# A decoder's second loop: metric scores in four 32-row tiles, and its orders rewritten

## The reference, cut to what matters

```python
metric_nkk = jnp.einsum('nij,nkj->nik', pre_metric_nkk, pre_metric_nkk)
proj_bwc = in_sequence_bwc @ W_proj.T
proj_bnwk = proj_bwc.reshape(b, w, N, K).transpose(0, 2, 1, 3)
qm_bnwk = jnp.einsum('bnwk,nkj->bnwj', proj_bnwk, metric_nkk)
scores_bnww = jnp.einsum('bnwk,bnvk->bnwv', qm_bnwk, proj_bnwk) / math.sqrt(K)
scores_bnww = scores_bnww * mask_ww          # lower triangle
nudged_bnwk = jnp.einsum('bnwv,bnvk->bnwk', scores_bnww, proj_bnwk)
nudged_bnwk = jnp.einsum('bnwk,nkj->bnwj', nudged_bnwk, transforms_nkk)
return nudged_bnwk.transpose(0, 2, 1, 3).reshape(b, w, c) @ W_mixer.T
```

## Time and profile before

| | |
|---|---|
| three runs | 1551.40, 1548.36, 1551.33 us, median 1551.33 |
| profiled execution | 1548.21 us, its span 1546.4 us |
| busy share of the span | PE 87%, PEld 57%, DVE 68%, ACT 34%, POOL 18% |
| TensorE's mean granted clock | 0.927 |
| largest lines of the chain that ended last | L824 10%, L1040 7%, L1099 6%, L934 6%, L759 4%, L988 4% |

### The profile page before, as it was taken

The page is one execution under the profiler, slowest core; times in us unless marked ns, Lnnn a source line. Parts: engine busy times, 40 slices in busy tenths (PEclk is TensorE's granted clock), DMA queues, the critical chain, the costliest instruction groups (busy, mean ns, idle before and its releaser), DMA issues.

```text
span 1546.4 us, 17959 instructions
## 1 busy us (share of the span) xinstructions
PE 1338.6 (87%) x7004; PEld 882.2 (57%) x7004; DVE 1052.5 (68%) x2018; ACT 523.8 (34%) x602; POOL 283.1 (18%) x188
## 2 busy tenths in 40 slices
PE   7999999988699997852276999999999999999874
PEld 4666676666444445421153567675757667666663
DVE  4688888863333336978724487787969788777774
ACT  2333333332233336966310323222333313232410
POOL 0111111110000001005400032323214032313240
PEclk9999999985799998975588999999999999999986
DMA  4000000000153211379612202011020200010000
GB/s 180 15 14 28 28 28 28 14 15 14 64 223 109 95 81 52 125 262 335 246 55 89 76 14 75 28 48 55 1 76 28 75 21 28 15 35 15 1 14 14
DMA packets 46000, 105.14 MB, mean 68 GB/s; under 512 B 10208, under 2 KB 30816, under 8 KB 42080
## 3 DMA queue, kind: packets, MB, share of 16 engines
q1 hardware_dynamic: 41760, 101.94, 18.4%
q10 hardware_dynamic: 4160, 2.10, 0.4%
HBM read 59.47 MB, written 44.56 MB: 67 GB/s over the span
## 4 chain that ended last, share of the span: by engine, by line
PE 72%; DVE 12%; ACT 7%; issue 4%; DMA 3%; POOL 2%; SPq 0%; POOLq 0%; ACTq 0%; DVEq 0%
PE ps L824 10%; PE ps L1040 7%; PE ps L1099 6%; PE ps L934 6%; PE ps L759 4%; PE ps L988 4%; PE ps L666 3%; PE ps L1073 3%; PE ps L775 2%; PE ps L739 2%; PE ps L948 2%; PE ps L1022 2%; PE ps L1115 2%; DVE arena L1895 2%; ACT arena L1187 2%
## 5 line engine op out<-in xcount | busy, mean ns | idle before, releaser
L824 PE MATMUL ps<-arena 128*128 128x512 f32 x384 | 166.5, 594 | 0.0
L1436 POOL TENSOR_TENSOR arena<-arena 128x4 f32<-128x4 f32 x48 | 49.2, 1025 | 409.1 <-DVE arena L1594 409.1
L824 PEld LDWEIGHTS ps<-arena 128*128 128x128 f32 x384 | 72.8, 191 | 88.8 <-issue 88.8
L1099 PE MATMUL ps<-arena 128*128 128x256 f32 x512 | 118.4, 385 | 5.6 <-ACT arena L1409 5.6
L1040 PE MATMUL ps<-arena 128*128 128x512 f32 x256 | 120.6, 601 | 0.0
L1895 DVE TENSOR_TENSOR arena<-ps,arena 128x1024 f32<-128x1024 f32 x64 | 78.1, 1220 | 52.2 <-PE ps L988 51.2
L1099 PEld LDWEIGHTS ps<-arena 128*128 128x128 f32 x512 | 97.0, 192 | 22.5 <-ACT arena L1409 8.4
L1498 POOL TENSOR_TENSOR arena<-arena 128x16 f32<-128x16 f32 x32 | 91.9, 2900 | 35.0 <-DVE arena L1924 35.0
L934 PE MATMUL ps<-arena 128*128 128x256 f32 x384 | 86.0, 385 | 13.5 <-DVE arena L1850 12.4
L1223 ACT ACTIVATE arena<-ps 128x512 f32<-128x512 f32 (+1 forms) x96 | 57.3, 597 | 105.4 <-PE ps L824 105.4
L934 PEld LDWEIGHTS ps<-arena 128*128 128x128 f32 x384 | 74.0, 193 | 27.6 <-issue 14.2
(11 more groups left out here) (240 smaller groups left out, 2602.8 us busy)
## 6 DMA issues: line engine op xcount, KB each, us to landing
up_scratch<-arena SPq DMA_DIRECT2D x8, 1536.0 KB, 6.0
arena<-up_scratch SPq DMA_DIRECT2D x8, 1536.0 KB, 9.7
v_scratch<-arena SPq DMA_DIRECT2D x8, 1536.0 KB, 6.4
arena<-v_scratch SPq DMA_DIRECT2D x7, 1536.0 KB, 7.0
arena<-x_scratch SPq DMA_DIRECT2D x16, 512.0 KB, 4.1
vw_scratch<-arena SPq DMA_DIRECT2D x16, 512.0 KB, 3.3
arena<-vw_scratch SPq DMA_DIRECT2D x8, 1024.0 KB, 4.8
arena<-x SPq DMA_DIRECT2D x8, 512.0 KB, 4.0
```

The lines of the kernel that those rows point to most:

```text
L824: last = mm(flat(2 + j), wt[:, k, j * P:(j + 1) * P], ffn_xt[:, par, k], start=k == 0, stop=k == NC - 1)
L1099: last = mm(flat(4)[:, C:2 * C], cos_pt[:, p], cos_vw[:, par, p], start=p == 0, stop=p == NP - 1)
```

## The change

The scores of a step m come from four matmuls on 32 partitions, 256 columns each (two heads), into the first halves of banks 3, 4, 5 and 6, in place of two on 64 partitions, 512 columns each, into all of banks 5 and 6. There are still eight steps a batch, one token tile each. The masked queries are stored twice, by a selector `duo16` made once (the sum of two columns of `quad16`), so `met_mask_queries` has two DVE instructions, not four. `met_mask` reads the half banks and still handles 1024 columns. The cosine values' output and the norms move from bank 4 to bank 2, turned probabilities and `cos_turn_x` from banks 2 and 3 to 3 and 4; new waits keep these apart from the scores (`met_scores(4)` on `cos_x_copied`, `cos_turn(0)` on the eighth mask, `cos_turn_x` on the fourth mask of the batch two on). `met_r` shares the memory of `met_ot`, hence a wait on `y4_ready` in `met_copy_o(0)`. `met_mix` waits for `met_p_ready` of the next batch, no longer for `dn_copied`, and `met_project` no longer waits for `met_added`: the next batch's projection comes ahead of the mix. The four lists are rewritten; the last two score steps and all but two output steps of a batch now lie in the same round as the first ones.

```diff
+        duo16 = small[:, 40:42]
...
-        met_qh = ar.take(4, T)
+        met_qh = ar.take(2, T)
-        met_s = ar.take(2, 2, 4, P)
+        met_s = ar.take(2, 4, 2, P)
-        met_r = ar.take(NT, C)
+        met_r = met_ot.rearrange("p a b -> p (a b)").rearrange("p (t c) -> p t c", t=NT)
...
+
+        def wait_ahead(eng, name, b, ahead, j, per):
+
+            if b.off + ahead < B:
+                eng.wait_ge(sig(name, per).sem, sig(name, per).at(b, per * ahead + j))
...
             def met_project(b, par):
                 wait(pe, "dn_copied", b)
-                wait_previous(pe, "met_added", b)
...
                         wait(pe, "met_states_ready", b)
                     else:
                         wait(pe, "met_masked", b, m, 8)
+                    if m == 4:
+                        wait_back(pe, "cos_x_copied", b, 2)
                     if t == 0:
                         wait(pe, "met_qh_ready", b, c + 1, 2)
-                    for r in range(2):
-                        lo, hi = 64 * r, 64 * r + 64
-                        last = mm(flat(5 + r), met_p[lo:hi, c, t * P:(t + 1) * P],
+                    for r in range(4):
+                        lo, hi = 32 * r, 32 * r + 32
+                        last = mm(flat(3 + r)[:, 0:256], met_p[lo:hi, c, t * P:(t + 1) * P],
                                   met_qh[lo:hi, :, t * P:(t + 1) * P], start=True, stop=True)
                     last.then_inc(sig("met_scored", 8).sem, 1)
                 return step
...
-                                      met_s[:, m % 2, g // 2, 2 * (g % 2) + odd], start=False,
+                                      met_s[:, m % 2, g, odd], start=False,
-                wait_next(pe, "dn_copied", b)
+                wait_next(pe, "met_p_ready", b)
...
-                        mm(flat(4)[32 * j:32 * j + 32], w["head_sel"][:, e], cos_sq[2 * j + e],
+                        mm(flat(2)[32 * j:32 * j + 32], w["head_sel"][:, e], cos_sq[2 * j + e],
...
             def cos_turn(t):
+                        wait_next(pe, "met_masked", b, 8, 8)
-                        last = tr(flat(2, 2)[:, p * P:(p + 1) * P], cos_s[:, t % 2, p * P:(p + 1) * P], ident)
+                        last = tr(flat(3, 2)[:, p * P:(p + 1) * P], cos_s[:, t % 2, p * P:(p + 1) * P], ident)
...
             def cos_turn_x(b, par):
-                turn_rows(2, y5, "cos_x_turned")
+                wait_ahead(pe, "met_masked", b, 2, 4, 8)
+                turn_rows(3, y5, "cos_x_turned")
...
             unrolled(pe, [
-                (2, met_out(4)), (2, met_scores(6)), (3, cos_scores(1)), (2, met_out(5)), (2, met_scores(7)),
-                (2, met_out(6)), (3, cos_scores(2)), (1, dn_turn), (2, met_out(7)), (3, cos_turn(0)), (2, met_mix),
-                (3, cos_out(0)), (3, cos_scores(3)), (1, met_project), (3, cos_turn(1)), (2, met_turn_x),
-                (3, cos_out(1)), (1, met_turn_p), (2, cos_query(0)), (1, met_queries), (2, cos_query(1)),
-                (0, dn_project(0)), (0, dn_project(1)), (0, dn_project(2)), (0, dn_project(3)), (3, cos_turn(2)),
-                (2, cos_query(2)), (3, cos_out(2)), (3, cos_turn(3)), (1, met_state), (3, cos_out(3)),
-                (2, cos_query(3)), (2, cos_query(4)), (1, met_scores(0)), (2, cos_query(5)), (1, met_scores(1)),
-                (1, met_out(0)), (2, cos_query(6)), (1, met_scores(2)), (2, cos_query(7)), (3, cos_turn_x),
-                (1, met_scores(3)), (1, met_out(1)), (3, spec_project), (1, met_out(2)), (2, cos_norm),
-                (1, met_scores(4)), (2, cos_turn_norms), (1, met_out(3)), (1, met_scores(5)), (2, cos_scores(0))])
+                (3, cos_scores(1)), (1, dn_turn), (2, met_out(6)), (2, met_out(7)), (1, met_project), (2, met_mix),
+                (3, cos_turn(0)), (3, cos_scores(2)), (3, cos_out(0)), (2, met_turn_x), (3, cos_scores(3)),
+                (1, met_turn_p), (3, cos_turn(1)), (1, met_queries), (3, cos_out(1)), (2, cos_query(0)),
+                (0, dn_project(0)), (0, dn_project(1)), (0, dn_project(2)), (0, dn_project(3)), (2, cos_query(1)),
+                (3, cos_turn(2)), (2, cos_query(2)), (3, cos_out(2)), (3, cos_turn(3)), (1, met_state),
+                (3, cos_out(3)), (2, cos_query(3)), (1, met_scores(0)), (2, cos_query(4)), (1, met_scores(1)),
+                (2, cos_query(5)), (1, met_out(0)), (1, met_scores(2)), (1, met_out(1)), (2, cos_query(6)),
+                (1, met_scores(3)), (2, cos_query(7)), (3, cos_turn_x), (1, met_out(2)), (1, met_out(3)),
+                (1, met_scores(4)), (3, spec_project), (2, cos_norm), (1, met_scores(5)), (2, cos_turn_norms),
+                (1, met_out(4)), (1, met_scores(6)), (2, cos_scores(0)), (1, met_out(5)), (1, met_scores(7))])
...
             def met_copy_o(c):
+                        wait_previous(act, "y4_ready", b)
...
             unrolled(act, [
+                (2, met_copy_x), (1, met_copy_pr), (3, cos_copy_pt(1)), (1, met_copy_halves), (3, cos_exp(2)),
+                (1, met_copy_q), (3, cos_exp(3)), (2, cos_copy_q(0)), (3, cos_copy_pt(2)), (2, cos_copy_q(1)),
+                (2, cos_copy_q(2)), (3, cos_copy_pt(3)), (2, cos_copy_q(3)), (2, cos_copy_q(4)), (2, cos_copy_q(5)),
+                (2, cos_copy_q(6)), (2, cos_copy_q(7)), (3, cos_copy_x), (2, cos_copy_norms), (1, met_copy_o(0)),
+                (0, dn_copy), (2, cos_exp(0)), (1, met_copy_o(1)), (0, met_copy_p), (2, cos_copy_pt(0)),
+                (2, cos_exp(1))])
...
             unrolled(pool, [
+                (3, cos_shift(2)), (3, cos_shift(3)), (3, cos_o_rstd(0)), (3, cos_o_rstd(1)), (3, cos_o_rstd(2)),
+                (0, loop2_rstd("dn")), (3, cos_o_rstd(3)), (3, loop2_rstd("cos")), (3, loop2_rstd("spec")),
+                (2, cos_norms(0)), (2, cos_norms(1)), (2, cos_norms(2)), (1, loop2_rstd("met")), (2, cos_norms(3))])
...
+            link(v.tensor_tensor(duo16, w["quad16"][:, 0:2], w["quad16"][:, 2:4], ALU.add))
...
-                    for h in range(4):
-                        last = v.tensor_scalar(met_qh[:, h], met_q[:, c], w["quad16"][:, h:h + 1], None, ALU.mult)
+                    for odd in range(2):
+                        last = v.tensor_scalar(met_qh[:, odd], met_q[:, c], duo16[:, odd:odd + 1], None, ALU.mult)
...
-                    v.tensor_tensor(met_s[:, m % 2].rearrange("p r h n -> p (r h) n"),
-                                    flat(5, 2).rearrange("p (h n) -> p h n", n=P),
-                                    w["causal"].unsqueeze(1).broadcast_to([P, 8, P]), ALU.mult)\
+                    v.tensor_tensor(met_s[:, m % 2], bank(3, 4)[:, :, 0:256].rearrange("p r (h n) -> p r h n", n=P),
+                                    w["causal"].unsqueeze(1).unsqueeze(1).broadcast_to([P, 4, 2, P]), ALU.mult)\
...
             unrolled(dve, [
+                (2, met_mask(7)), (3, cos_max(0)), (3, cos_shift(0)), (3, cos_scale(1)), (3, cos_sum(0)),
+                (3, cos_divide(0)), (3, cos_max(1)), (3, cos_shift(1)), (2, met_add), (3, cos_scale(2)),
+                (2, met_finish), (3, cos_sum(1)), (3, cos_divide(1)), (3, cos_max(2)), (3, cos_o_stats(0)),
+                (0, dn_round(0)), (3, cos_scale(3)), (0, dn_round(1)), (3, cos_max(3)), (0, dn_round(2)),
+                (3, cos_sum(2)), (0, dn_round(3)), (3, cos_divide(2)), (3, cos_o_stats(1)), (3, cos_sum(3)),
+                (3, cos_divide(3)), (1, met_mask_queries(0)), (3, cos_o_add(0)), (0, dn_add), (3, cos_o_stats(2)),
+                (3, cos_o_add(1)), (3, cos_o_add(2)), (1, met_mask_states), (3, cos_o_stats(3)), (1, met_mask(0)),
+                (3, cos_o_add(3)), (1, met_mask(1)), (3, cos_stats), (1, met_mask(2)), (3, cos_finish),
+                (1, met_mask(3)), (2, met_floor), (1, met_mask_queries(1)), (1, met_mask(4)), (0, dn_finish),
+                (3, spec_add), (1, met_mask(5)), (2, cos_floor), (3, spec_finish), (1, met_mask(6)),
+                (2, cos_scale(0))])
```

More of the change, by code:

```diff
@@ L1060, in cos_turn_norms @@
                 for t in range(NT):
-                    last = tr(flat(4)[:, t * P:(t + 1) * P], cos_nt[:, t], ident)
+                    last = tr(flat(2)[:, t * P:(t + 1) * P], cos_nt[:, t], ident)
                 last.then_inc(sig("cos_n_turned").sem, 1)
@@ L1393, in cos_copy_norms @@
                 wait(act, "cos_q_normed", b)
-                f(all_of(cos_nt), flat(4), ACT.Copy).then_inc(sig("cos_n_copied").sem, 1)
+                f(all_of(cos_nt), flat(2), ACT.Copy).then_inc(sig("cos_n_copied").sem, 1)
             def cos_exp(t):
@@ L1414, in cos_copy_x @@
                 wait_previous(act, "spec_done", b)
-                f(all_of(xt5), flat(2, 2), ACT.Copy).then_inc(sig("cos_x_copied").sem, 1)
+                f(all_of(xt5), flat(3, 2), ACT.Copy).then_inc(sig("cos_x_copied").sem, 1)
             unrolled(act, [
-                (3, cos_copy_norms), (2, met_copy_o(0)), (3, cos_exp(0)), (1, dn_copy), (2, met_copy_o(1)),
```

(7 more changed lines are left out.)

25 lines of the change are left out of this document (5 added, 20 removed).

## The result

The changed kernel takes 1546.34 us (median of 20 runs, 1542.86 to 1549.70), the kernel before beside it 1549.13 (20 runs, 1547.16 to 1551.50). The ratio is 0.9979, with an interval of [0.9972, 0.9986]: faster by 2.8 us by the medians and 3.3 by the ratio (2.2 to 4.3 by its interval), where I had said some 10. The profiled execution took 1545.12 us, with a span of 1543.3. Two of ten executions in e5 (1678 and 6343 us) and one of the kernel before beside them (1699) were in a slower state, and every median and ratio in this document is of the fast runs alone.

The account below looks back on a forecast made before the run. It took TensorE to bound full rounds, and chains the fill and drain; 1.0 - 1.3 - 6.2 - 1.9 - 1.3 = -9.7 took 1548.21 to 1538.5, or 1541.6 from the median; it said 1541, range 1530 to 1552.

Parts of the forecast that it names:

- fill: Second loop's start: batch 0's mix stays at about 846, `met_copy_pr` loses its cover; +1.0 us (-2 to +4).
- the second round of scores: Round after the fill: a full round's -1.6 less 0.3 for missing cosine and spectral steps; -1.3 us.
- four full rounds: Second loop's complete rounds, each going from 87.07 to 85.5 us; -6.2 us for the four.
- the last-scores round: Round with the last batch's scores: no down projection, same waits, last masks no longer late; -1.9 us.
- the drain: Loop's end: mix freed early, but `cos_turn(0)` put ahead of `cos_scores(2)`; -1.3 us (-3 to +2).
- Score step, 0.64: `met_scores`: eight instructions, four abreast in two waves, 0.64 us in place of 1.06; eight steps save 3.4 a round.
- Rival C: Score step: only two row tiles run abreast, price stays 1.06; about +14, 1565 us; chance 0.06.
- The new waits, 2.95 idle: TensorE's waits in a full round: 2.95 us idle in place of 1.03, +1.9; largest 1.37 ahead of `met_mix`.
- The clock stays at 1.00 in full rounds: Sign named in advance: TensorE's granted clock remains 1.00 throughout the second loop's full rounds.
- no long wait ahead of `met_turn_x`: Sign in the round: no idle time over 0.5 us ahead of `met_turn_x`, or VectorE's lateness is at work.
- Rival D: Round's head: VectorE late with a mask or `cos_scale(2)`; 1551 us at 1.5 more a round, 1558 at 2.5; chance 0.19.
- rival B: TensorE's new waits are hidden: 1524 us with full columns, 1532 with half the waits gone; chance 0.13.

Follow-up runs that it names:

- e5: Changed kernel with `cos_turn(0)` ahead of `met_mix` in every round: 1550.89 us, ratio 1.0012 to the kernel before.
- e4: Changed kernel's orders and waits with the old 64-row score tiles, four masked-query instructions and their mask: 1569.10 us, ratio 1.0125 to the kernel before.
- e8: Changed kernel with `met_mix` straight behind `met_out(7)` in every round, `met_project` behind `cos_out(0)`, both ends mended: 1534.42 us, ratio 0.9908 to the kernel before.
- e1: Changed kernel with three pairs put back in the fill's pass alone, among them `met_mix` ahead of `met_project`: 1536.57 us, ratio 0.9922 to the kernel before.
- e3: Changed kernel with six matmuls that nobody reads behind batch 0's mix in the fill, order unchanged: 1541.84 us, ratio 0.9954 to the kernel before.
- e2: Changed kernel with `cos_scores(2)` ahead of `cos_turn(0)` in the last round alone: 1539.88 us, ratio 0.9941 to the kernel before.
- e6: Changed kernel with the edits of e1 (fill) and e2 (last round) together: 1536.66 us, ratio 0.9925 to the kernel before.
- e10: Kernel before with twenty idle matmuls in the waits of its last round alone: 1542.49 us, ratio 0.9958 to the kernel before.

## Why the prediction was wrong

The sign was right and the size was not: I said -9.7 for the profiled executions, and -3.1 was measured. The time itself, 1546.34, lies in the range said, 1530 to 1552, but that is no merit of the sum. Its parts were off by +10.4 at the two ends and by -3.8 in between, and it started from a median of three runs, 1551.33, that lies 2.2 above that of twenty. By its terms, in equal work: fill +6.4 against +1.0 said, the second round of scores -1.9 against -1.3, four full rounds -8.3 against -6.2, the last-scores round -3.0 against -1.9, the drain +3.7 against -1.3.

- *Score step, 0.64.* Right: 0.65, four row tiles abreast. Rival C (step 1.06) is out. An estimate by the factor of the Trainium skill, "TensorE: Matmul & The Clock Gate", Part 3 (Packing small matmuls), had been 0.56; the row says 0.65. The Trainium skill gives that factor for 512 columns; the step here has 256. By e4 a step saves 0.35 of the round's length, a little less than the 0.41 from start to start (1.06 to 0.65): TensorE's busy time falls by 3.1, and its idle time rises by 0.3, 0.24 of it ahead of `cos_scores(1)`, which has less cover. From before to after a round's busy time fell by 3.12, where -3.5 was said.
- *The new waits, 2.95 idle.* Right in kind and in order, too large by 0.9: measured 2.08. The handover by ScalarE's copy ahead of the mix is there with 1.21; from the end of one step's slot to the next start it is 1.46, 1.37 was said. `met_project` waited hardly at all (0.23 said), and `met_queries` and `cos_scores(1)` less than said. So the waits cost 0.9 less than said and the steps saved 0.4 less, and a full round gained 2.07 and not 1.57. The round, 85.00, is on the lower edge of the 85 to 86 named. Two slips of the working are small: the time up to `cos_scores(1)`, 0.37 and 1.21, adds to 1.58 and not 1.63, and four rounds at -1.6 make -6.4 and not -6.2. A third bears on the drain: in the earlier trace rows the last three slices fall (8, 7, 4), not two.
- *The clock stays at 1.00 in full rounds; no long wait ahead of `met_turn_x`* in them. Right. Rival D is out for full rounds, and rival B too: 2.08 of idle time stand in a round, and e5 and e8 show the waits changing their place.
- *The fill, "+1.0 (from -2 to +4)".* This is the first step that failed, outside its own bounds. I saw that `met_project` now comes ahead of the mix and counted when the mix would start (846 said, 848.03 measured), and stopped there. What stood behind the mix I did not walk: the project had been the cover of the chain that the mix starts, 5.88 of idle time now. e1 shows that it is this order (66.3 to 58.2; 7.2 by the means), e3 that about 3.5 of it are the clock. The earlier trace rows showed 0.81 in the fill already; I still priced every step there at its full-clock row.
- *The drain, "-1.3 (-3 to +2)".* The second that failed, also outside. I named the edit that costs (`cos_turn(0)` ahead of `cos_scores(2)`, "worse") but gave it no price of its own, and let it be outweighed by the mix's early release. The trace of before had it: in the last round `cos_scores(2)` started 10.2 behind `cos_scores(0)` and the turn 13.8, so the turn put first can move the scores by up to 3.6. e2 gives 4.2 for it in its own pair of profiles, 2.8 by the means. By the mean of five profiles the changed drain is 2.7 longer than before and not 3.7, still outside the bounds.

A round that occurs four times was worked out wait by wait; each end, which occurs once, got a line. The errors of the two ends, +5.4 and +5.0, are each larger than what four full rounds were off by (-2.1).

Open: how much the unchanged code's clock in the fill and the drain differs from one execution to the next for reasons of its own, and so the split between order and clock to better than about 2 us; which of e1's three reversed pairs counts most; and why e6 is no better than e1.

## What to carry to other kernels

When an order written for the full round is remade, walk the passes that fill and drain the loop step by step as well: there a step's cover is the one or two steps that are left, and a reversed pair can cost more than the steady rounds give; keep another order for these passes. Price each wait there twice, once in idle time and once in the slower steps behind it. In a queue that issues in order a wait that is covered at one place can come out at the next reader of the same chain (e5), so count the chain's length and not the wait. And a step moved ahead to cover a wait is itself a wait where its own chain is late, as in e5's partly filled rounds.

## What the runs showed of the hardware

- While TensorE idled for 5.88 us in the fill, the granted clock fell to the lower of its two levels, 1.2 GHz, and the three steps behind took about twice their time (1.97 for 1.06, 3.75 for 1.88). With the same gap filled by matmuls that nobody reads (e3), the clock was 1.00 and the steps 1.09, 1.06 and 1.99. It cost 3.4 to 4.7 us there; the low clock in the drain costs 5 to 7.
- Such work paid even on the kernel before: twenty idle matmuls took the last round from 68.9 to 62.2 (e10).
- A shorter wait was followed by the lower level too: behind 2.34 us of idle time ahead of the mix at 1415.52 the granted clock fell from 1.00 to 0.50 just before 1417, with TensorE at work again since 1415.52, and the mix took 5.41 in place of 3.69.
- The clock's pattern at the loop's ends is not the same in every execution of the same code: `dn_project(1)` to batch 0's mix took 45.2 in one profile of the changed kernel's code and 43.0 in two others (e2, e3). A gain of 2 us there cannot be read from a single profile.
- Eight matmuls of 256 columns in four 32-row tiles cost 0.65 us a step, where four of 512 columns in two 64-row tiles cost 1.06. As an estimate from these and from 0.21 for 256 columns, that is two waves of 0.21 and some 0.2 for the change of tiling, which did not shrink with the tile.
